# Pairing the score products and the transposes of two units in the first three attentions of a four-layer gated cross-attention model

## The chip, the cores and the metric

The kernel runs on one core of a Trainium2 chip. The metric is the time of one execution on the device, in microseconds; it is given as the median of several executions. The profile and the trace come from one further execution.

## The reference

Four layers, each a gated cross-attention and a gated feed-forward part, on an input x of 4 x 256 tokens with 128 features and a context of the same shape:

```python
x = x + tanh(g_xattn[0]) * L0_xattn(layernorm(x), ctx, ctx, adj, mask, ...)
x = x + tanh(g_ffn[0])   * L0_ffn(layernorm(x), ...)
x = x + tanh(g_xattn[1]) * L1_xattn(layernorm(x), ctx, ctx, bias, padding, ...)
x = x + tanh(g_ffn[1])   * L1_ffn(layernorm(x), ...)
x = x + tanh(g_xattn[2]) * L2_xattn(layernorm(x), ctx, ctx, mask, padding, ...)
x = x + tanh(g_ffn[2])   * L2_ffn(layernorm(x), ...)
x = x + tanh(g_xattn[3]) * L3_xattn(ctx, layernorm(x), ...)
x = x + tanh(g_ffn[3])   * L3_ffn(layernorm(x), ...)
```

The first three attentions have the same form, with 16 heads of 8 features, and differ in what is added to the scores and masked:

```python
q = heads(query @ Wq.T + bq); k = heads(key @ Wk.T + bk); v = heads(value @ Wv.T + bv)
scores = einsum('bhqd,bhkd->bhqk', q, k) * 8 ** -0.5 + bias        # 256 x 256 for each batch and head
weights = softmax(where(masked, -inf, scores), axis=-1)
out = einsum('bhqk,bhkd->bhqd', weights, v)                        # then @ Wo.T + bo
```

## The kernel before

The program is written out by hand for five engines, each of which issues its own list of instructions in order and waits for the others on semaphores. The stages follow one another: attention, feed-forward, and so on. The change concerns `attention(a)` of TensorE for a = 0, 1, 2.

In each of these attentions the work is cut into 64 units, one for each batch and head (`UNITS`; a group is four units with four heads of one batch, a batch is 16 units). A loop runs over steps t, on each engine with the same numbering, and in step t each engine does its part for a unit that lies a fixed number of steps back:

- TensorE, unit t: two score matmuls in bf16 of 128 x 256 each (line 998) into one of three PSUM banks (`SBANK`). They wait until VectorE is through with unit t - 3, which had the same bank.
- VectorE, unit t: adds the mask and bias and takes the negated row maximum, two custom instructions that write SBUF (line 1444).
- ScalarE, unit t: the exponential with the row sum, two instructions of 128 x 256 (line 715).
- TensorE, unit t - 3 (`LAG`): four transposes of the exponentials in f32 (line 1018) into one of three further banks (`TBANK`). They wait for the exponentials of that unit and for the copy of the unit that had the bank.
- Copy of the transposed unit t - 3 from PSUM to SBUF, by VectorE (line 1456), and for every fourth unit (those with number 2 in their group) by ScalarE (line 727).
- TensorE, every fourth step from 8 on (`PV_T`) and the step behind it: the product with V of a group, in two parts of four matmuls of 32 x 256 (line 1033). The first part waits until all four units are copied and until ScalarE has emptied the only bank for it.
- ScalarE, every fourth step from 9 on (`OTR_T`): copy of that product out of its bank (line 735).
- TensorE, every fourth step from 13 on (`SEL_T`): eight small matmuls that spread the reciprocal row sums (line 1050); VectorE multiplies the two (line 1466).
- TensorE and VectorE, at steps 27, 43, 59 and 75 (`OUT_T`), once for each batch: the output projection (lines 1061 and 1064) and its addition to x (line 1351).

The order within one step is the order of this list. Since each engine's list is in order, an instruction that waits holds back all that stands behind it. The lines that set the three lags and the banks:

```python
LAG, PV_T, OTR_T, SEL_T, OUT_T = 3, 8, 9, 13, 27
def SBANK(n):
    return bank[(0, 1, 7)[n % 3]]
def TBANK(n):
    return bank[(2, 3, 5)[n % 3]]
def loop_rings(ra, rb):
    return Ring((6,), s_fa, s_ea, ra.n, ra.n), Ring((4,), s_fb, s_eb, rb.n, rb.n)
```

Of the kernel before, what the change touches and what calls it, by code (L numbers as in the profile page):

```python
# [46 lines left out]
UNITS = 64  # L47
# [71 lines left out]
LAG, PV_T, OTR_T, SEL_T, OUT_T = 3, 8, 9, 13, 27  # L119
# [7 lines left out]
def program(nc, x_in, ctx_in, ctxT_in, w_in, adj_in, mask_in, pad_in, wint_in, out):  # L127
    with ExitStack() as stack:  # L128
# [719 lines left out]
        def _(pe):  # L848
# [87 lines left out]
            def attention(a):  # L936
                three = a == 3
                base = UNITS * a
                if not three:
                    if a == 0:  # L940
                        keys(0)
                    for c in range(NC):
                        bk = ra.fill(pe)
                        for i in range(4):
                            t = 4 * c + i
# [37 lines left out]
                la, lb = loop_rings(ra, rb)  # L983
                otr_at = {}
                for t in range(UNITS + SEL_T):
                    if t < UNITS:
                        n = base + t
                        b, j, g = t // 16, t % 4, t // 4 % 4
                        if n >= 3:

                            pe.wait_ge(s_max, 2 * n - 4)
                        bk = SBANK(n)
                        if t % 16 == 0:

                            pe.wait_ge(s_qs[min(b, 2)], 32 * (a + 1))
                        h = 4 * g + j
                        for q in range(2):
                            mm = nc.tensor.matmul(bk[:, q * S:(q + 1) * S],  # L998
                                                  QS[:, h, b * S + q * P:b * S + (q + 1) * P],
                                                  KS[:, h // 2, b * S:(b + 1) * S], start=True, stop=True)  # L1000
                        mm.then_inc(s_s, 1)
                    u = t - LAG
                    if 0 <= u < UNITS:
                        n = base + u
                        pe.wait_ge(s_exp, 2 * n + 2)
                        if n >= 3:

                            m = n - 3
                            if m % 4 == 2:
                                pe.wait_ge(s_te, m // 4 + 1)  # L1010
                            else:
                                pe.wait_ge(s_to, m // 4 * 3 + min(m % 4 + 1, 3))
                        bk = TBANK(n)
                        for kt in range(2):
                            for q in range(2):
                                o = kt * S + q * P
                                i = q * S + kt * P
                                mm = nc.tensor.transpose(bk[:, o:o + P], P_OF(n)[:, i:i + P], ident)  # L1018
                        mm.then_inc(s_t, 1)
# [936 lines left out]
```

## Time and profile before

| | us |
|---|---|
| median of 3 executions | 953.72 (953.38 to 954.16) |
| profiled execution | 955.74 |
| its span, first to last instruction | 954.0 |
| TensorE busy | 739.0 (77%) |
| VectorE busy | 629.7 (66%) |
| ScalarE busy | 531.1 (56%) |
| GpSimd busy | 211.9 (22%) |
| mean granted TensorE clock | 0.879 |

The shares are averages over stages that differ. The three loops of the change lie at 43.8 to 138.7, 188.6 to 283.2 and 564 to 659 us of the trace, some 285 us of the 954. Within a stage, an engine's idle time counts only where the others wait for it. A row of the trace in order of time gives the start, the duration from the first to the last of the instructions merged in it, engine, line, operation and tiles, the number of instructions, and in brackets the idle time of the engine just before and what ended it. The granted clock is a share of 2.4 GHz, so that 0.50 is 1.2 GHz. A matmul of f32 that is no transpose counts as two instructions in the trace, and as one in the listing of the program further down.

### The profile page before, as it was taken

The page shows a single profiled execution, that of the slowest core. Times are in us where ns is not written, and L with a number is a line of the kernel's source. Part 1 is how long each engine was busy: PE and PEld are TensorE (multiplying, and loading weights), DVE is VectorE, ACT ScalarE, POOL GpSimd, SP SyncE. Part 2 cuts the span into 40 slices and gives each one's busy share as a digit, 9 for nine tenths or more (in the row PEclk, how much of TensorE's full clock was granted, in tenths as well). Part 3 has the DMA queues.
Part 4 walks back from the last instruction along what each step waited for, and adds up shares of the span by engine and source line. Part 5 has one row for each costly group of instructions (what it writes and reads, how often), then busy time and mean ns, then how long its engine had stood idle before and what let it go on. Part 6 is the DMA issues. An engine that isn't in the chain of part 4 may idle for free. (4 is left out here: it accounts for less than half of the span.)

```text
span 954.0 us, 14468 instructions
## 1 busy us (share of the span) xinstructions
PE 739.0 (77%) x4720; PEld 415.6 (44%) x4720; DVE 629.7 (66%) x1861; ACT 531.1 (56%) x1376; POOL 211.9 (22%) x161
## 2 busy tenths in 40 slices
PE   4599973399975776877783559995899999969987
PEld 2266652166653222322331236664533666644322
DVE  3699957399963557686786569986532656634543
ACT  2398841198843775775674149882367655522211
POOL 7702004100004345364364630001010000000000
PEclk9699995599995987888896759998899999988999
DMA  7992040420000000000000190000000000000000
GB/s 285 181 345 68 3 67 1 103 31 2 2 2 0 0 1 0 0 1 0 1 0 0 26 173 2 2 3 23 1 0 1 1 1 1 1 0 1 1 0 23
DMA packets 22060, 32.29 MB, mean 34 GB/s; under 512 B 1761, under 2 KB 15713, under 8 KB 21217
## 3 DMA queue, kind: packets, MB, share of 16 engines
q1 hardware_dynamic: 21984, 31.36, 13.1%
q8 instruction: 39, 0.64, 0.3%
q14 instruction: 37, 0.29, 0.1%
HBM read 21.39 MB, written 9.96 MB: 33 GB/s over the span
## 5 line engine op out<-in xcount | busy, mean ns | idle before, releaser
L715 ACT ACTIVATE RING<-RING,NMX 128x256 f32<-128x256 f32 x384 | 190.6, 500 | 54.1 <-DVE NMX L1444 53.5
L1444 DVE CUSTOM_DVE_ANT_0 RING<-bank,ADJM 128x256 f32<-128x256 f32 x384 | 143.4, 413 | 22.7 <-DMA scratch<-RING 21.7
L1018 PE MATMUL bank<-W,RING 128*128 128x128 f32 x768 | 120.3, 281 | 15.7 <-ACT RING L727 14.0
L495 POOL TENSOR_TENSOR small<-small 128x8 f32<-128x8 f32 (+2 forms) x13 | 17.6, 1360 | 463.8 <-DVE small L1335 463.8
L1018 PEld LDWEIGHTS bank<-W,RING 128*128 128x128 f32 x768 | 91.3, 145 | 28.1 <-ACT RING L715 24.5
L998 PE MATMUL bank<-ARENA 128*128 128x256 bf16 x384 | 77.5, 289 | 28.8 <-DMA ARENA<-scratch 23.6
L1456 DVE COPY RING<-bank 128x512 f32<-128x512 f32 x144 | 98.6, 686 | 1.2 <-PE bank L1018 0.8
L857 PE MATMUL bank<-XT,W 128*128 128x512 f32 (+3 forms) x138 | 78.0, 706 | 7.2 <-ACT XT L611 5.1
L857 PE MATMUL bank<-ARENA 128*128 128x512 f32 (+2 forms) x164 | 62.2, 522 | 23.8 <-DVE ARENA L1537 10.2
L857 PE MATMUL bank<-ARENA,W 128*128 128x512 f32 (+4 forms) x104 | 54.4, 648 | 27.7 <-DVE ARENA L1657 10.9
L590 POOL TENSOR_TENSOR ARENA<-ARENA,RING 128x512 f32<-128x512 f32 x38 | 59.8, 1583 | 67.4 <-DVE RING L1627 35.5
L715 ACT ACTIVATION_READ_ACCUMULATOR RING<-RING,NMX 128x1 f32 x384 | 72.8, 190 | 0.0
L627 ACT ACTIVATE RING<-bank,NMX 128x512 f32<-128x512 f32 x64 | 43.4, 683 | 41.9 <-PE bank L922 21.2
L1033 PE MATMUL bank<-RING,ARENA 128*32 128x256 f32 x768 | 60.7, 390 | 2.7 <-DVE RING L1456 2.5
L1376 DVE TENSOR_REDUCE NMX<-bank 128x1 f32<-128x512 f32 x64 | 39.4, 678 | 31.9 <-PE bank L889 31.9
L1595 DVE TENSOR_SCALAR RING<-bank,W 128x512 f32<-128x512 f32 x36 | 27.0, 751 | 48.7 <-PE bank L1126 46.6
L998 PEld LDWEIGHTS bank<-ARENA 128*128 128x128 bf16 x384 | 31.1, 102 | 63.7 <-issue 38.0
L1126 PE MATMUL bank<-ARENA 128*128 128x512 f32 x72 | 39.4, 690 | 18.2 <-DVE RING L1602 15.0
L857 PEld LDWEIGHTS bank<-ARENA 128*128 128x128 f32 (+1 forms) x164 | 28.2, 196 | 55.3 <-issue 27.0
L857 PEld LDWEIGHTS bank<-XT,W 128*128 128x128 f32 (+2 forms) x138 | 26.9, 219 | 44.6 <-issue 23.6
L857 PEld LDWEIGHTS bank<-ARENA,W 128*128 128x128 f32 (+4 forms) x104 | 17.2, 186 | 66.2 <-issue 24.2
L842 ACT ACTIVATE RING<-bank 128x512 f32<-128x512 f32 x24 | 14.3, 597 | 56.6 <-PE bank L857 41.9
(240 smaller groups left out, 1395.6 us busy)
## 6 DMA issues: line engine op xcount, KB each, us to landing
scratch<-ARENA SPq DMA_DIRECT2D x18, 256.0 KB, 3.1
ARENA<-scratch SPq DMA_DIRECT2D x6, 768.0 KB, 10.6
W<-in_weights SPq DMA_DIRECT2D x1, 2564.0 KB, 21.2
scratch<-RING SPq DMA_DIRECT2D x36, 64.0 KB, 3.2
ARENA<-scratch SPq DMA_DIRECT2D x12, 192.0 KB, 3.7
scratch<-RING SPq DMA_DIRECT2D x18, 128.0 KB, 2.7
ARENA<-scratch SPq DMA_DIRECT2D x6, 384.0 KB, 7.0
W<-in_weights SPq DMA_DIRECT2D x2, 1024.0 KB, 13.8
```

The costliest lines, as they stand in the source:

```text
L590: nc.gpsimd.tensor_tensor(acc[:, half(c)], acc[:, half(c)], term, ALU.add).then_inc(s_sum, 1)
L627: nc.scalar.activation(LP_OF(u), bank[j][:, :], ACT.Exp, bias=NMX[:, u:u + 1], accum_out=SUMS[:, u:u + 1]).then_inc(l_exp, 1)
L715: nc.scalar.activation(P_OF(n)[:, q * S:(q + 1) * S], S_OF(n)[:, q, :], ACT.Exp, bias=NMX[:, 2 * t + q:2 * t + q + 1], scale=-1.0, accum_o ...
L857: mm = nc.tensor.matmul(bk[0:m, 0:rhs.shape[-1]], lhsT, rhs, start=(i == 0), stop=(i == len(terms) - 1))
L998: mm = nc.tensor.matmul(bk[:, q * S:(q + 1) * S], QS[:, h, b * S + q * P:b * S + (q + 1) * P], KS[:, h // 2, b * S:(b + 1) * S], start=Tru ...
L1018: mm = nc.tensor.transpose(bk[:, o:o + P], P_OF(n)[:, i:i + P], ident)
L1033: mm = nc.tensor.matmul(pv[PAD * j:PAD * j + PAD, 0:S], V[:, 2 * b + part, f:f + PAD], PT_OF(base + 4 * G + j)[:, part * S:(part + 1) * S] ...
L1126: nc.tensor.matmul(bank[u % 3][:, :], *control(u, 1), start=True, stop=True).then_inc(s_fs, 1)
L1376: nc.vector.tensor_reduce(NMX[:, u:u + 1], bank[j][:, :], AX.X, ALU.max, negate=True).then_inc(l_max, 1)
L1444: nc.vector.tensor_tensor_reduce(out=S_OF(n)[:, q, :], in0=SBANK(n)[:, q * S:(q + 1) * S], in1=ADJM[:, b, q, :], scale=-1.0, scalar=BIG, o ...
L1456: nc.vector.tensor_copy(PT_OF(n), TBANK(n)[:, :]).then_inc(s_to, 1)
L1595: nc.vector.tensor_scalar(SP_OF(u), bank[u % 3][:, :], be2[:, u % (NE + 1), 1:2], CLAMP, ALU.add, ALU.min).then_inc(s_mn, 1)
```

## The change

The score matmuls of units t and t + 1 are both issued in the even step t, and none in odd steps. The transposes, which in step t were those of unit t - 3, are now issued in odd steps only, for the units t - 4 and t - 3. All waits stay the same for each unit; the other engines' lists are not changed. Everything else in a step stays in its place, so the first part of a group's product with V, which falls into an even step, now directly follows the scores.

```diff
                 for t in range(UNITS + SEL_T):
-                    if t < UNITS:
-                        n = base + t
-                        b, j, g = t // 16, t % 4, t // 4 % 4
+                    for v in (t, t + 1) if t % 2 == 0 and t < UNITS else ():
+                        n = base + v
+                        b, j, g = v // 16, v % 4, v // 4 % 4
                         if n >= 3:
 
                             pe.wait_ge(s_max, 2 * n - 4)
                         bk = SBANK(n)
-                        if t % 16 == 0:
+                        if v % 16 == 0:
...
-                    u = t - LAG
-                    if 0 <= u < UNITS:
+                    for u in (t - 4, t - 3) if t % 2 == 1 else ():
+                        if not 0 <= u < UNITS:
+                            continue
                         n = base + u
                         pe.wait_ge(s_exp, 2 * n + 2)
```

The following listings show TensorE's matmuls in the order of the program: L998 are scores (two for a unit), L1018 transposes (four for a unit), L1033 the products with V, L1050 the spreading of the row sums. The change adds a line, so these are L1019, L1034 and L1051 in the second listing of each pair.

First, TensorE at the start of the first loop, before:

```order
L998 MATMUL bank<-ARENA 128x256 x8
L1018 MATMUL bank<-W,RING 128x128 x4
L998 MATMUL bank<-ARENA 128x256 x2
L1018 MATMUL bank<-W,RING 128x128 x4
L998 MATMUL bank<-ARENA 128x256 x2
L1018 MATMUL bank<-W,RING 128x128 x4
```

and after:

```order
L998 MATMUL bank<-ARENA 128x256 x8
L1019 MATMUL bank<-W,RING 128x128 x4
L998 MATMUL bank<-ARENA 128x256 x4
L1019 MATMUL bank<-W,RING 128x128 x8
L998 MATMUL bank<-ARENA 128x256 x4
L1019 MATMUL bank<-W,RING 128x128 x8
```

The transposes of unit 1 stood behind the scores of unit 4 and now stand behind those of units 4 and 5; those of unit 3 stood behind unit 6's scores and now stand behind units 6's and 7's.

Second, TensorE in a full group of four units (steps 4m to 4m + 3), before:

```order
L998 MATMUL bank<-ARENA 128x256 x2
L1018 MATMUL bank<-W,RING 128x128 x4
L1033 MATMUL bank<-RING,ARENA 32x256 x4
L998 MATMUL bank<-ARENA 128x256 x2
L1018 MATMUL bank<-W,RING 128x128 x4
L1033 MATMUL bank<-RING,ARENA 32x256 x4
L1050 MATMUL bank<-W,SUMS 32x128 x8
L998 MATMUL bank<-ARENA 128x256 x2
L1018 MATMUL bank<-W,RING 128x128 x4
L998 MATMUL bank<-ARENA 128x256 x2
L1018 MATMUL bank<-W,RING 128x128 x4
```

and after:

```order
L998 MATMUL bank<-ARENA 128x256 x4
L1034 MATMUL bank<-RING,ARENA 32x256 x4
L1019 MATMUL bank<-W,RING 128x128 x8
L1034 MATMUL bank<-RING,ARENA 32x256 x4
L1051 MATMUL bank<-W,SUMS 32x128 x8
L998 MATMUL bank<-ARENA 128x256 x4
L1019 MATMUL bank<-W,RING 128x128 x8
```

The first part of the product with V stood behind the transposes of the group's first pair and now stands ahead of them; in both halves of the group one unit's scores have passed one unit's transposes.

Third, TensorE behind the last scores of the first loop, before:

```order
L998 MATMUL bank<-ARENA 128x256 x2
L1018 MATMUL bank<-W,RING 128x128 x8
L1033 MATMUL bank<-RING,ARENA 32x256 x4
L1018 MATMUL bank<-W,RING 128x128 x4
L1033 MATMUL bank<-RING,ARENA 32x256 x4
L1050 MATMUL bank<-W,SUMS 32x128 x8
L1018 MATMUL bank<-W,RING 128x128 x4
```

and after:

```order
L998 MATMUL bank<-ARENA 128x256 x4
L1019 MATMUL bank<-W,RING 128x128 x8
L1034 MATMUL bank<-RING,ARENA 32x256 x4
L1019 MATMUL bank<-W,RING 128x128 x8
L1034 MATMUL bank<-RING,ARENA 32x256 x4
L1051 MATMUL bank<-W,SUMS 32x128 x8
L1019 MATMUL bank<-W,RING 128x128 x4
```

The transposes of unit 61 stood ahead of the first product here and now stand behind it, with those of unit 62.

## Rows read from the trace of the kernel before

**Rows 1.** Stretch: length, busy us PE, PEld, DVE, ACT, POOL, granted clock. First loop, its start.
```profile
43.80:138.70 94.90, 86.28 (x970) 62.61 (x970) 83.09 (x344) 77.96 (x288) 12.00 (x8) 0.96 0.46 129
43.80:50.60 6.80, 5.44 (x25) 4.53 (x26) 6.06 (x29) 5.98 (x24) 5.65 (x4) 0.50 1.18 181
```

**Rows 2.** Waits of VectorE in the first loop: total us, times, longest.
```profile
DVE XN L1466 <- PE bank L1050: 4.6, 7, 1.6
```

**Rows 3.** VectorE in order of time, steps 33 to 38: start, us, instruction.
```profile
86.81 0.42 DVE L1466 TENSOR_TENSOR XN<-XT,bank 128x256 f32<-128x256 f32 x1
...
91.76 0.42 DVE L1466 TENSOR_TENSOR XN<-XT,bank 128x256 f32<-128x256 f32 x1
92.11 0.42 DVE L1444 CUSTOM_DVE_ANT_0 RING<-bank,ADJM 128x256 f32<-128x256 f32 x1
...
92.81 0.69 DVE L1456 COPY RING<-bank 128x512 f32<-128x512 f32 x1
```

**Rows 4.** TensorE in order of time, steps 36 to 39.
```profile
88.65 0.63 PE L1018 MATMUL bank<-W,RING 128*128 128x128 f32 x4 [0.92 <-ACT RING L727]
89.21 0.64 PE L1033 MATMUL bank<-RING,ARENA 128*32 128x256 f32 x8
89.78 0.39 PE L998 MATMUL bank<-ARENA 128*128 128x256 bf16 x2
90.01 0.60 PE L1018 MATMUL bank<-W,RING 128*128 128x128 f32 x4
90.54 0.64 PE L1033 MATMUL bank<-RING,ARENA 128*32 128x256 f32 x8
90.99 0.62 PE L1050 MATMUL bank<-W,SUMS 128*32 128x128 f32 x16
91.55 0.39 PE L998 MATMUL bank<-ARENA 128*128 128x256 bf16 x2
91.78 0.60 PE L1018 MATMUL bank<-W,RING 128*128 128x128 f32 x4
92.21 0.38 PE L998 MATMUL bank<-ARENA 128*128 128x256 bf16 x2
```

**Rows 5.** ScalarE in order of time, steps 33 and 34.
```profile
87.93 0.58 ACT L727 ACTIVATE RING<-bank 128x512 f32<-128x512 f32 x1
88.41 0.37 ACT L735 ACTIVATE XT<-bank 128x256 f32<-128x256 f32 x1
...
89.56 0.19 ACT L715 ACTIVATION_READ_ACCUMULATOR RING<-RING,NMX 128x1 f32 x1
```

**Rows 6.** TensorE and VectorE in order of time at the starts of the loops.
```profile
49.23 0.63 PE L998 MATMUL bank<-ARENA 128*128 128x256 bf16 x2
49.66 1.06 PE L1018 MATMUL bank<-W,RING 128*128 128x128 f32 x4
...
193.01 0.69 DVE L1456 COPY RING<-bank 128x512 f32<-128x512 f32 x1
...
194.59 0.42 DVE L1444 CUSTOM_DVE_ANT_0 RING<-bank,ADJM 128x256 f32<-128x256 f32 x1 [0.21 <-ACT RING L715]
...
568.45 1.06 PE L1018 MATMUL bank<-W,RING 128*128 128x128 f32 x4
```

**Rows 7.** TensorE and VectorE in order of time around the second batch end.
```profile
100.83 0.61 DVE L1351 SCALAR_TENSOR_TENSOR X<-bank,small,X 128x128 f32<-128x128 f32 x2 [1.02 <-PE bank L1064]
...
103.26 0.62 PE L1050 MATMUL bank<-W,SUMS 128*32 128x128 f32 x16
...
103.95 0.42 DVE L1466 TENSOR_TENSOR XN<-XT,bank 128x256 f32<-128x256 f32 x1 [0.55 <-PE bank L1050]
```

**Rows 8.** TensorE and VectorE in order of time behind the last scores.
```profile
128.06 0.64 PE L1033 MATMUL bank<-RING,ARENA 128*32 128x256 f32 x8
...
128.63 0.66 PE L1018 MATMUL bank<-W,RING 128*128 128x128 f32 x4
...
130.91 0.69 DVE L1456 COPY RING<-bank 128x512 f32<-128x512 f32 x1
```

## The prediction

> **What bounds the kernel now.** I read the busy time of the first attention loop first, then the waits of VectorE in it, then the order of time on three engines in one group of four units, then the same at the loop's start, at a batch end and at its end. Units are named by number: S(n) the two score matmuls, M(n) VectorE's mask-add-and-minimum, E(n) ScalarE's exponentials, T(n) the four transposes, C(n) the copy to SBUF, PV0 and PV1 the two halves of a group's product with V, SEL the product that spreads the row sums, OTN VectorE's multiplication behind it.
>
> The loop of the first attention takes 94.90 us, in which VectorE is busy 83.09, TensorE 86.28 and ScalarE 77.96 [rows 1]; the two other loops look alike. VectorE hardly waits inside it: 4.6 us in seven waits for SEL [rows 2], and 1.02 us at each of the three batch ends inside the loop [rows 7]. The rest of its idle time lies behind the last scores. So between the batch ends **VectorE sets the pace**, one group of four units in 4.95 us (OTN at 86.81 to OTN at 91.76, with M directly behind, [rows 3]), and TensorE only has to be in time. It just is: SEL starts at 90.99, an OTN can start 0.69 behind a SEL (103.26 and 103.95, [rows 7]), so 91.68, and does at 91.76; S(38) starts at 91.55 and M(38), which needs it complete, at 92.11 [rows 3, 4]. A group in which TensorE comes later than now is therefore paid in full, one in which it comes earlier brings nothing, except where VectorE waits for it.
>
> **The change part by part.** No instruction is added or taken away. Of every two steps the order S(2k), T(2k-3), S(2k+1), T(2k-2) becomes S(2k), S(2k+1), T(2k-3), T(2k-2); so S(2k+1) passes one T, and PV0, which stood behind T(2k-3), now stands ahead of it.
>
> *Full groups.* Take steps 36 and 37. Before: T(33) at 88.65, 0.14 behind the copy of unit 30 on ScalarE (87.93 and 0.58), then PV0 0.56 later, S(37) 0.57, T(34) 0.23, PV1 0.53, SEL 0.45 [rows 4, 5]. Now S(37) goes into the 0.92 us that TensorE idles ahead of T(33); it waits for M(34) only, which directly follows the OTN at 86.81 and is through some 1.1 us behind it. PV0 comes next, and needs its bank emptied: ScalarE's copy for the group before ends at 88.41 + 0.37 = 88.78 [rows 5]. With the same 0.14, PV0 starts at 88.92, T(33) 0.57 later (PV0 to T(62) is 0.57 in [rows 8]) at 89.49, T(34) 0.43 later at 89.92 (T(35) to S(39) is 0.43, [rows 4]; E(34) is complete at 89.56 + 0.19 = 89.75, so that wait is hidden), PV1 0.53 later at 90.45, SEL 0.45 later at 90.90. That is **0.09 earlier** than 90.99. T(35) then starts at 90.90 + 0.56 + 0.23 + 0.23 = 91.92 and ends 0.60 later at 92.52, while its copy starts at 92.81 [rows 3]: hidden, with 0.3 left. T(33) ends at 90.1, 0.8 later than before; its copy comes one step behind that of unit 32 and not before 90.4: hidden, with 0.3 left. So full groups cost 0.
>
> The 0.14 is a handoff from ScalarE to TensorE as the row shows it. The Trainium skill (Advanced Engine Details and Errata, Network/Comms) gives 50 to 100 ns for reading a semaphore; by that PV0 would start at 88.83 to 88.88, the chain would be 0.04 to 0.09 shorter still, and the sum below 0.4 to 0.9 us lower. The sum takes 0.14.
>
> *Where VectorE waits.* The batch result's matmuls start when the same T(4m) is through as before, so the 0.09 is gained in each of 3 x 3 waits of 1.02, and in the first of the seven waits for SEL: 10 x 0.09 = **0.9 us gained**. Behind a batch end TensorE issues S(44), S(45), PV0, T(41), T(42), PV1, SEL in place of S(44), T(41), PV0, S(45), T(42), PV1, SEL: the same pieces. C(41), which followed M(44) at once, comes some 0.44 later, but VectorE then waits 0.55 for SEL anyway [rows 7], so this is hidden, and only just. Bounds: 0 to 1.8.
>
> *Start of the loops.* There TensorE runs at 1.2 GHz (granted clock 0.50 in the first 6.80 us, and with 0.96 over the whole loop it is 1.00 behind them, [rows 1]) and is the slower engine. T(1) and T(3) now stand behind one more pair of scores, 0.43 at that clock (49.23 to 49.66, [rows 6]). First loop: T(3) starts at 50.09 in place of 49.66 and runs partly at 2.4 GHz, since the clock rises at 50.6. All at the low clock it would end 0.43 later, all at the high one (0.60 for 1.06) 0.03 earlier; I take 0.24 for it and for C(3) directly behind. Second loop: C(1), at 193.01, comes 0.41 later; two steps further the wait of 0.21 ahead of M(6) at 194.59, and what is idle beside it, swallow 0.2 to 0.3 of that. I take 0.15. Third loop: T(1) starts 0.43 behind 568.45, at 568.88, and meets the rising clock too, so some 0.17. Nothing behind these gives them back, since the stalls further on are reached through the same engines. Together 0.24 + 0.15 + 0.17 = **0.6 us**, between 0 and 1.2.
>
> *End of the loops.* In step 64 the order is PV0, T(61) where it was T(61), PV0. PV0 starts at 128.06, behind a copy on VectorE that does not move, and T(61) used to be done by then (the pair T(60), T(61) stood ahead). Now T(61) stands between PV0 and T(62), and everything behind it (T(62) at 128.63, PV1, SEL, T(63), C(63) at 130.91) comes 0.43 later [rows 8]. E(63) does not hold it: it follows M(63), which is not moved. Behind C(63) all is one chain up to the next layer's normalisation. 3 x 0.43 = **1.3 us**, and I see no cover: bounds 1.2 to 1.3.
>
> Sum: 1.3 + 0.6 - 0.9 = +1.0 us. The profiled execution took 955.74 us (span 954.0), 2.02 more than the median of 953.72; the sum is a difference, so I forecast 956.7 for a profiled execution and **954.7 for the median**. A measurement of this kernel tells about 0.2% from no change, which is 1.9 us; so this is no change that can be told.
>
> **The rivals.**
>
> *PV0 hands over late (slower).* PV0 now gates T, T, PV1 and SEL, and it waits for the last thing that ScalarE does in its group. If the handoff is above 0.14 + 0.09 = 0.23, SEL and S(38) come later than now and VectorE pays in every full group. At 0.30 it is 0.07 in each of 12 groups x 3, 2.5 us; the 0.9 gained at batch ends is gone and 9 x 0.07 = 0.6 is lost there: 1.0 + 0.9 + 2.5 + 0.6 = +5.0, so 958.7. For it: slack behind S(38) is nil, and T(34) has only 0.17 to spare behind E(34). Against it: both waits for ScalarE in [rows 4, 5] end 0.14 behind it. 18 in 100.
>
> *The pieces pack more tightly (faster).* A T followed by PV takes 0.53, followed by S 0.43; PV followed by a waiting S takes 0.57, by SEL 0.45 [rows 4]. If in the new order the 0.10 and the 0.12 fall away around PV0, the chain to a batch end and the one from it to SEL each lose 0.22: 9 x 0.44 = 4.0 us more gained, so +1.0 - 4.0 = -3.0, 950.7. For it: [rows 7] show the places at which it would count. Against it: the 0.57 also stands in front of a T in [rows 8]. 10 in 100.
>
> *The clock falls.* Were the new pauses of TensorE (at most 0.7 us, where today's are 0.92) to drop it to 1.2 GHz in the loops, the pair of scores would take 0.43 as in [rows 6] in place of 0.23 as in [rows 4], all else twice as long too, and a group's own chain of some 4.4 us (4 x 0.66 for S and T, 1.76 for the rest) 8.8 in place of VectorE's 4.95: 48 x 3.9 = 185 us more, 1140. The Trainium skill (TensorE: Matmul & The Clock Gate, A second HAM failure mode: psum-queue depth-cycling) says that short idles between groups of matmuls that cycle through banks can make the clock swing; by that rule this rival would be the outcome. The trace stands against it: the granted clock stays at 1.00 behind the loop's start [rows 1], with such idles in every group. 1 in 100.
>
> *Clock edges move.* The clock rises at another point of each loop's start and of the stages between, since the pauses around it shift by some tenths. Three starts at one bound or the other are 1.2 us apart, and the stages between have such edges too. up to 1.5 us either way, the width of my forecast.
>
> **How the numbers follow.** The forecast has 71 in 100: of these 55 within 0.2%, 11 above (starts at their upper bound and no gain at the batch ends: 1.3 + 1.2 = 2.5) and 5 below. With the rivals: faster by over 0.2% 5 + 10 = 15, within 55, slower 11 + 18 + 1 = 30. The range goes down to 952.4 and up to 958.0; it leaves out most of the tight packing, the upper half of the late handoff and the clock, about 19 in 100.
>
> **What would show it.** In the profile after: C(63) to the loop's end unchanged but C(63) about 0.4 later behind PV0; T(61) and T(62) in one row of eight; in full groups OTN to OTN still 4.95 and no wait on VectorE; PV0 0.14 behind ScalarE's copy of the bank; batch-end waits of 0.9 in place of 1.02; behind a batch end a wait of VectorE ahead of C(41) in place of part of that for SEL. Wrong if VectorE waits for SEL, scores or transposes in groups where it does not now, or if the loops are shorter than before.

## The result, and the profile after

The changed kernel took a median of 955.04 us (952.91 to 958.23, 20 runs), the kernel before on the same chips 953.62 us (951.15 to 954.48, 20 runs). The ratio is 1.002 with an interval of 1.0011 to 1.0030: some 1.0 to 2.9 us slower, 1.9 by the ratio itself and 1.4 by the medians. The forecast of 954.7 us holds within half a microsecond. Its second half, "no change that can be told", does not quite: the interval excludes no change, though the loss is no larger than the 0.2% that the prediction took as its bound for telling one.

The profiled execution of the changed kernel has a span of 953.0 us, one less than before (954.0), at a mean granted clock of 0.881 (0.879 before). The busy times on the profile's page are nearly those of before (739.0, 415.6, 629.7, 531.1 and 211.9 us):

```profile
PE 739.4 (78%) x4715; PEld 417.3 (44%) x4720; DVE 630.7 (66%) x1861; ACT 530.0 (56%) x1376; POOL 211.8 (22%) x161
```

A shorter span and a longer median do not contradict each other. The stages that the change does not touch took 3.4 us less in this one execution than in that of before, and the three loops 2.4 us more. The untouched stages run the same program in both, so their difference is scatter between executions. The loops must therefore be read on their own. I cut each loop at VectorE's rows, by start times: from its first mask instruction to the first batch result (the addition to x, line 1351, now 1352), from there to the third batch result, and from there to the last.

| us | to the first batch result, loops 1 / 2 / 3 | first to third | third to last | sum of three loops |
|---|---|---|---|---|
| before | 34.82 / 34.55 / 34.24 | 44.39 | 15.09 | 282.06 |
| after | 35.20 / 34.62 / 34.62 | 44.42 | 15.58 | 284.46 |

The two middle columns are the same in all three loops to within 0.02. So the +2.40 consist of +0.83 in the stretches that hold the starts, 3 x 0.03 in the middle, and 3 x 0.49 = +1.47 at the ends.

The changed kernel in the first loop (columns as in [rows 1]: stretch, length, busy time of PE, PEld, DVE, ACT, POOL, granted clock):

```profile
43.80:139.00 95.20, 86.96 (x970) 63.24 (x970) 82.96 (x343) 77.71 (x288) 11.90 (x8) 0.96 0.46 128
```

The clock is 0.96 as in [rows 1]; TensorE now idles ahead of PV0 and not ahead of T(33), and this did not lower it. Its waits (engine, tile and line that waited, what it waited for: total, times, longest), VectorE's and one of TensorE's:

```profile
DVE X L1352 <- PE bank L1065: 6.3, 4, 3.2
DVE XN L1467 <- PE bank L1051: 3.1, 3, 1.6
DVE RING L1457 <- PE bank L1019: 2.2, 6, 0.4
PE bank L1034 <- ACT XT L735: 3.8, 7, 0.9
```

The profile lists three waits of VectorE for SEL where it listed seven ([rows 2]), and six for transposes. It lists none under 0.15 us. One full group of four units, three engines in order of time (start, us from the first to the last of the merged instructions, engine, line, operation, tiles, count, idle before and what ended it):

```profile
87.00 0.42 DVE L1467 TENSOR_TENSOR XN<-XT,bank 128x256 f32<-128x256 f32 x1
...
88.59 0.37 ACT L735 ACTIVATE XT<-bank 128x256 f32<-128x256 f32 x1
...
89.11 0.64 PE L1034 MATMUL bank<-RING,ARENA 128*32 128x256 f32 x8 [0.55 <-ACT XT L735]
...
89.68 1.09 PE L1019 MATMUL bank<-W,RING 128*128 128x128 f32 x8
...
90.70 0.64 PE L1034 MATMUL bank<-RING,ARENA 128*32 128x256 f32 x8
...
91.15 0.62 PE L1051 MATMUL bank<-W,SUMS 128*32 128x128 f32 x16
91.71 0.61 PE L998 MATMUL bank<-ARENA 128*128 128x256 bf16 x4
91.95 0.41 DVE L1467 TENSOR_TENSOR XN<-XT,bank 128x256 f32<-128x256 f32 x1
```

OTN to OTN is 4.95 as before, and VectorE waits nowhere in it. PV0 waits for ScalarE's copy and starts 0.15 behind its end (88.59 + 0.37 = 88.96), 2.11 behind OTN, as forecast. SEL, however, is 4.15 behind OTN; it was 4.18 ([rows 3, 4]), and 4.09 was expected. The group behind this one takes 4.95 (91.95 to 96.90), where it took 4.97 before (91.76 to 96.74): in the kernel before M(38) waited 0.02 for its scores, which stand behind SEL, and now it does not. The earlier TensorE brings that much and no more.

A batch end:

```profile
100.99 0.61 DVE L1352 SCALAR_TENSOR_TENSOR X<-bank,small,X 128x128 f32<-128x128 f32 x2 [1.03 <-PE bank L1065]
...
101.99 1.09 PE L1019 MATMUL bank<-W,RING 128*128 128x128 f32 x8
...
102.69 0.69 DVE L1457 COPY RING<-bank 128x512 f32<-128x512 f32 x1 [0.41 <-PE bank L1019]
...
103.02 0.64 PE L1034 MATMUL bank<-RING,ARENA 128*32 128x256 f32 x8
...
103.47 0.62 PE L1051 MATMUL bank<-W,SUMS 128*32 128x128 f32 x16
...
104.16 0.42 DVE L1467 TENSOR_TENSOR XN<-XT,bank 128x256 f32<-128x256 f32 x1
```

The wait for the batch result is 1.03, where [rows 7] had 1.02. Behind it the wait of 0.55 for SEL is no longer listed and one of 0.41 for the transposes of the pair stands in its place: the copy of unit 41, which followed its mask instructions at once, now waits. SEL still holds OTN all the same. OTN starts 0.69 behind SEL (103.47 to 104.16) as in [rows 7], with 0.10 of waiting left, too short for the list. OTN comes 3.17 behind the batch result, where it came 3.12, because SEL comes 2.48 behind it and not 2.43 ([rows 7]).

Behind the last scores of the loop:

```profile
128.31 0.64 PE L1034 MATMUL bank<-RING,ARENA 128*32 128x256 f32 x8 [0.58 <-DVE RING L1457]
128.88 1.09 PE L1019 MATMUL bank<-W,RING 128*128 128x128 f32 x8
129.90 0.64 PE L1034 MATMUL bank<-RING,ARENA 128*32 128x256 f32 x8
130.35 0.62 PE L1051 MATMUL bank<-W,SUMS 128*32 128x128 f32 x16
...
131.60 0.69 DVE L1457 COPY RING<-bank 128x512 f32<-128x512 f32 x1
```

The transposes of units 61 and 62 are one row of eight between the two products, and the last copy comes 131.60 - 128.31 = 3.29 behind PV0, where it came 130.91 - 128.06 = 2.85 ([rows 8]): 0.44 later.

### The profile page after: what moved, and what is told of

The parts are those of the page before. It is cut to its first block and busy times, and to the rows that moved or that the text cites. A ratio compares the mean times of both kernels' runs of the same rounds, so it can differ in the third digit from the quotient of the medians.

```text
span 953.0 us, 14463 instructions
## 1 busy us (share of the span) xinstructions
PE 739.4 (78%) x4715; PEld 417.3 (44%) x4720; DVE 630.7 (66%) x1861; ACT 530.0 (56%) x1376; POOL 211.8 (22%) x161
## 5 line engine op out<-in xcount | busy, mean ns | idle before, releaser
L1019 PE MATMUL bank<-W,RING 128*128 128x128 f32 x768 | 107.0, 283 | 1.6 <-ACT RING L715 1.6
L1019 PEld LDWEIGHTS bank<-W,RING 128*128 128x128 f32 x768 | 88.2, 145 | 23.0 <-ACT RING L715 17.8
L998 PE MATMUL bank<-ARENA 128*128 128x256 bf16 x384 | 64.3, 289 | 28.3 <-DMA ARENA<-scratch 22.9
L1034 PE MATMUL bank<-RING,ARENA 128*32 128x256 f32 x768 | 60.7, 389 | 18.1 <-ACT XT L735 11.5
L998 PEld LDWEIGHTS bank<-ARENA 128*128 128x128 bf16 x384 | 33.3, 102 | 50.6 <-issue 31.8
```

Of the source, the lines that this page charges most:

```text
L998: mm = nc.tensor.matmul(bk[:, q * S:(q + 1) * S], QS[:, h, b * S + q * P:b * S + (q + 1) * P], KS[:, h // 2, b * S:(b + 1) * S], start=Tru ...
L1034: mm = nc.tensor.matmul(pv[PAD * j:PAD * j + PAD, 0:S], V[:, 2 * b + part, f:f + PAD], PT_OF(base + 4 * G + j)[:, part * S:(part + 1) * S] ...
```

## The experiments

My theory said where the time goes: into the starts, where TensorE is still slow and is the bound, and into the ends, where all is one chain; full groups were to cost nothing, and the batch ends to give a little back. The rivals put it into the full groups or the clock. Each experiment changes nothing but the order of TensorE's list. Ratios are against the kernel before, run on the same chip, and need not be the quotient of two medians. The stretches are those of the table above, from one profiled execution of each kernel. The middle and the last stretch repeat to 0.02 us in the three loops of an execution; the starts do not. The intervals of most ratios overlap, so which part of the order costs what is read from the stretches, and the ratios only confirm the size.

| kernel | median us | ratio (interval) | starts, loops 1 / 2 / 3 | first to third | third to last | loops |
|---|---|---|---|---|---|---|
| end single | 955.29 | 1.0010 (1.0000 to 1.0021) | 34.47 / 34.75 / 34.50 | 44.42 | 15.47 | 283.39 |
| full groups only | 954.93 | 1.0008 (0.9995 to 1.0020) | 34.44 / 34.77 / 34.77 | 44.43 | 15.46 | 283.67 |
| scores only | 952.71 | 0.9995 (0.9984 to 1.0006) | 34.38 / 34.24 / 34.21 | 44.20 | 15.13 | 280.82 |
| transposes only | 958.27 | 1.0043 (1.0028 to 1.0058) | 35.05 / 35.49 / 35.54 | 44.69 | 15.54 | 286.76 |
| single from 60 | 954.02 | 1.0009 (0.9999 to 1.0019) | 34.97 / 34.61 / 34.59 | 44.42 | 15.14 | 282.86 |
| scores from 8 | 954.07 | 1.0004 (0.9991 to 1.0016) | 34.24 / 33.97 / 33.95 | 44.20 | 15.14 | 280.16 |
| product behind pair | 956.60 | 1.0037 (1.0025 to 1.0050) | 35.09 / 35.24 / 35.22 | 44.48 | 15.40 | 285.20 |
| scores and late product | 948.93 | 0.9958 (0.9941 to 0.9974) | 33.96 / 33.96 / 33.95 | 43.61 | 14.98 | 277.64 |
| late product only | 951.08 | 0.9983 (0.9969 to 0.9997) | 34.82 / 34.80 / 34.24 | 43.90 | 14.97 | 280.46 |

### The end alone undone

On the changed kernel, transposes of one unit per step once the scores are through:

```diff
-                    for u in (t - 4, t - 3) if t % 2 == 1 else ():
+                    for u in (t - 3,) if t >= UNITS else (t - 4, t - 3) if t % 2 == 1 else ():
```

> The change, but behind the last scores (steps 64 on) TensorE issues the transposes as before: T(61) ahead of PV0. Loop lengths are from the first mask-and-minimum of VectorE to the last addition to x, summed over the three loops: 282.06 us before, 284.46 after the change. Theory (the cost lies at the starts and ends of the loops, full groups are free): the end is back at its old length, 0.49 less in each loop, sum 283.0; in time about +0.9 us over the kernel before in place of +1.4 to +2.4. Rival (the cost is spread over the full groups and batch ends): the sum stays at 284.0 or more. Rival (nothing but scatter): no length moves by a fixed amount.

The last stretch came down from 15.58 to 15.47 only, not to 15.09, and the sum to 283.39, not to 283.0, so my account of the end was not complete. TensorE behind the last scores of the first loop, and ScalarE's last steps before it:

```profile
125.72 0.51 ACT L715 ACTIVATE RING<-RING,NMX 128x256 f32<-128x256 f32 x1 [0.69 <-DVE NMX L1445]
...
126.72 0.57 ACT L727 ACTIVATE RING<-bank 128x512 f32<-128x512 f32 x1
...
127.44 0.63 PE L1019 MATMUL bank<-W,RING 128*128 128x128 f32 x4 [0.30 <-ACT RING L727]
128.00 0.64 PE L1034 MATMUL bank<-RING,ARENA 128*32 128x256 f32 x8
```

The transposes of unit 61 stand ahead of PV0 again, but now they are late themselves: they wait for the bank that ScalarE copies out (126.72 and 0.57), and PV0 waits behind them. ScalarE is late because of the third batch end, at step 60. There the pair's transposes come behind PV0, VectorE waits 0.4 us for them as in the batch end shown above, and ScalarE behind it waits 0.69 for VectorE (125.72), where the kernel further down that undoes the order from step 60 on waits 0.19. From there to unit 58's copy ScalarE has no idle time left to make this good. In the changed kernel this cannot be seen, since PV0 does not stand behind a copy of ScalarE there. The end thus had **two covers for one loss**: lifting one shows the other.

### Only the full groups changed

In addition, scores and transposes of single units up to step 7:

```diff
-                    for v in (t, t + 1) if t % 2 == 0 and t < UNITS else ():
+                    for v in (t,) if t < 8 else (t, t + 1) if t % 2 == 0 and t < UNITS else ():
-                    for u in (t - 3,) if t >= UNITS else (t - 4, t - 3) if t % 2 == 1 else ():
+                    for u in (t - 3,) if t < 8 or t >= UNITS else (t - 4, t - 3) if t % 2 == 1 else ():
```

> Pairs only from step 8 to step 63, the first eight steps and all behind step 63 as before. Theory: both costs are gone, the sum of the loop lengths is 282.1 (within 0.3), the time that of the kernel before within 0.1%; the wait of VectorE behind a batch end still stands ahead of its copy (0.40) and no longer at the multiplication. Rival (spread over groups and batch ends): 283.5 to 284.5.

The sum, 283.67, missed the 282.1 of the theory and lies where the rival had it. The rival is wrong all the same: the middle, which holds the full groups and batch ends, is 44.43 against 44.39, 0.12 in three loops. The end is 15.46, as in the run before, which makes 1.1. The starts look no better in the table (34.44, 34.77, 34.77, against 34.82, 34.55, 34.24 of the kernel before, which has the same order there), so start stretches of single executions can't be compared as they stand: the clock's rise falls at another point each time. For each start, the table gives how long the granted clock stayed at 1.2 GHz behind the first mask, and how far the first OTN lies behind that mask:

| order up to step 7 | us at 1.2 GHz, and first mask to first OTN |
|---|---|
| single (before, this kernel, late product) | 4.33: 15.18; 4.47: 15.18; 5.32: 15.40; 5.42: 15.48; 6.76: 15.74; 6.85: 15.75; 6.93: 15.73; 7.33: 15.73; 7.41: 15.76 |
| both paired (after, end single, single from 60) | 4.34: 15.42; 4.44: 15.46; 4.62: 15.55; 4.65: 15.57; 5.19: 15.57; 5.24: 15.57; 6.29: 15.70; 6.75: 15.92; 7.38: 16.15 |

Two things are in it. A clock that rises 3 us later costs a start 0.55 us in the single order (15.18 to 15.73) and 0.73 in the paired one (15.42 to 16.15). And at nearly the same rise the paired order costs 0.2 to 0.4 more: 0.24 at 4.3 us, 0.28 at 4.4, 0.17 at 5.2 to 5.3, 0.18 at 6.8 and 0.39 at 7.4. The mean is 0.25, so my estimate for three starts is 0.75 us; the 0.83 of the table hold a little of the clock's scatter too.

### One half of the change at a time

Scores paired, transposes single:

```diff
-                    for u in (t - 4, t - 3) if t % 2 == 1 else ():
+                    for u in (t - 3,):
```

> Only the scores are paired; the transposes stand in their old steps, so PV0 is behind T(33) again and S(37) no longer between PV0 and T(34). Theory: TensorE reaches the row-sum product 0.18 earlier in a full group, which brings nothing, since VectorE sets the pace (4.95 us a group); the starts cost what they cost in the change (0.8 in all), the ends nothing: sum 282.9, time +0.8 us over before. Rival (an earlier TensorE is worth something in each group): a sum below 281.

The full groups take 4.95, the wait for the batch result is 0.92, the middle is 44.20 and the end 15.13. Group and batch end of this kernel, TensorE and VectorE:

```profile
86.33 0.42 DVE L1467 TENSOR_TENSOR XN<-XT,bank 128x256 f32<-128x256 f32 x1
...
90.36 0.62 PE L1051 MATMUL bank<-W,SUMS 128*32 128x128 f32 x16
...
91.28 0.42 DVE L1467 TENSOR_TENSOR XN<-XT,bank 128x256 f32<-128x256 f32 x1
...
100.21 0.61 DVE L1352 SCALAR_TENSOR_TENSOR X<-bank,small,X 128x128 f32<-128x128 f32 x2 [0.92 <-PE bank L1065]
```

SEL is 4.03 behind OTN, 0.15 earlier than in the kernel before, and the wait for the batch result is 0.10 shorter: what I had forecast for the whole change (0.09 in each) does happen, with this half. In the groups themselves 0.02 is gained, in the one of four that took 4.97. The sum of 280.82 missed the 282.9 of the theory and lies under the 281 of the rival, but not for the rival's reason. Of the 1.24 less than before, 0.57 are in the middle, from the shorter waits for the batch result, and 0.78 in the starts (the ends take 0.12 more). In the starts the clock rose earlier in this execution (5.53, 4.38 and 4.31 us behind the first mask, against 6.85, 5.42 and 4.33 before). What the paired scores cost a start is read further down.

Then transposes paired, scores single:

```diff
-                    for v in (t, t + 1) if t % 2 == 0 and t < UNITS else ():
+                    for v in (t,) if t < UNITS else ():
```

> Only the transposes are paired; S(37) stands between PV0 and T(33). PV0 still waits for ScalarE's copy of its bank, and now S, T, T, PV1 and the row-sum product follow it: that product comes about 0.2 us later than in the kernel before. Theory (TensorE is just in time, later is paid in full): 0.12 to 0.19 in each of some 40 groups, 5 to 7 us, beside the 2.3 of starts and ends: sum 289 to 292, time +7 to +10 us, groups of 5.1 in place of 4.95, and VectorE waits for the row-sum product in full groups. Rival (there is slack in the groups): sum 284.5, as the change.

This is the rival in which TensorE is late in a full group, made to happen:

```profile
86.59 0.42 DVE L1467 TENSOR_TENSOR XN<-XT,bank 128x256 f32<-128x256 f32 x1
...
90.92 0.62 PE L1051 MATMUL bank<-W,SUMS 128*32 128x128 f32 x16
91.61 0.42 DVE L1467 TENSOR_TENSOR XN<-XT,bank 128x256 f32<-128x256 f32 x1
92.04 0.42 DVE L1445 CUSTOM_DVE_ANT_0 RING<-bank,ADJM 128x256 f32<-128x256 f32 x1
...
95.87 0.62 PE L1051 MATMUL bank<-W,SUMS 128*32 128x128 f32 x16
96.66 0.42 DVE L1467 TENSOR_TENSOR XN<-XT,bank 128x256 f32<-128x256 f32 x1
```

SEL is 4.33 behind OTN (86.59 to 90.92), 0.15 later than before. OTN follows 0.69 behind it, 5.02 behind the last and 0.07 later than the 4.95 of before; the other 0.08 had been slack. They are paid one instruction further: M(38) starts 0.43 behind OTN (91.61 to 92.04) and not 0.35 ([rows 3]), since its scores stand behind the late SEL. So the group that begins there takes 5.05 in place of 4.97, although its own SEL (95.87) does not hold the next OTN, which follows 0.79 behind it. Together the lateness of 0.15 is paid in full, as the prediction said of a late group. But it is paid once in a batch, over two groups. The group behind a batch end has slack (5.06 before, 5.05 here), the group that holds the next batch end waits for the batch result anyway, and the middle rose by 0.30 in two batches, not by the several microseconds that I had expected. The sum of 286.76 thus lies between the theory (289 to 292) and the rival (284.5). The ratio of 1.0043 (4.1 us) agrees with the loops (+4.70).

### The end once more, single from step 60 on

If both covers are known, undoing the pairs from the third batch end on must give the end back:

```diff
-                    for u in (t - 4, t - 3) if t % 2 == 1 else ():
+                    for u in (t - 3,) if t >= 60 else (t - 4, t - 3) if t % 2 == 1 else ():
```

> The change, but from step 60 on the transposes stand in their old steps (in the run before this only from step 64 on, which left the end at 15.47 us, from the third batch result to the last, against 15.09 before and 15.58 with the change). Theory: the end has two covers that the change takes away one by one. Behind the third batch end the transposes of unit 57 come late, VectorE and through it ScalarE fall back by 0.4, and ScalarE's copy of unit 58 then holds back the product and all behind it; undoing the order from step 60 removes both: end 15.1 to 15.2. Middle (first to third batch result) unchanged at 44.42. Rival (undoing the end never helps, the 0.4 come from the scores of units 61 and 63 being early): end 15.45 as in the run before.

TensorE and ScalarE, where the run above had its wait of 0.30:

```profile
126.40 1.48 PE L1019 MATMUL bank<-W,RING 128*128 128x128 f32 x12
126.53 0.58 ACT L727 ACTIVATE RING<-bank 128x512 f32<-128x512 f32 x1
128.01 0.64 PE L1034 MATMUL bank<-RING,ARENA 128*32 128x256 f32 x8
```

Three units' transposes run in one piece, with no wait among them. The last stretch is 15.14, against 15.58 changed and 15.09 before. So 0.44 of the end's 0.49 come from the transposes paired in steps 60 to 65.

### Scores paired, but not at the start

On the changed kernel:

```diff
-                    for v in (t, t + 1) if t % 2 == 0 and t < UNITS else ():
+                    for v in (t,) if t < 8 else (t, t + 1) if t % 2 == 0 and t < UNITS else ():
-                    for u in (t - 4, t - 3) if t % 2 == 1 else ():
+                    for u in (t - 3,):
```

> Candidate that may beat both: scores paired from step 8 on, the first eight steps and all transposes as in the kernel before. Theory: middle 44.20 as in the run with only the scores paired (44.39 before), end 15.13 (15.09 before), start as before at the same length of the slow clock (first row-sum multiplication 15.2 to 15.8 us behind the first mask, by when the clock rises). Each loop 0.2 to 0.3 us shorter than before, 0.7 us in all, 0.9993: at or under what can be told. Rival: no shorter than before, 1.0000 or above, because the start gives it back.

The loops are the shortest so far (280.16, 1.9 less than before), and the ratio of 1.0004 with an interval from 0.9991 to 1.0016 does not show it. It only excludes a gain above 0.9 us. This is the one kernel whose loops and ratio differ by more than 1.5 us. Part of the 1.9 is the clock's: it rose 5.37, 4.59 and 4.53 us behind the first mask here, and 6.85, 5.42 and 4.33 before. The third loop's start, at nearly the same rise, is 0.29 shorter (33.95 against 34.24); with that for each start my estimate of the gain is 3 x (0.29 + 0.19 - 0.05) = 1.3 us. That is still above what the timing allows, and I leave it at that: a gain of this size is at the edge of what these runs can tell.

The starts can be priced here once more, since this kernel differs from the one with only the scores paired in the first eight steps alone. The first OTN lies 15.31, 15.03 and 15.03 us behind the first mask here, and 15.45, 15.32 and 15.28 there, with rises at 5.53, 4.38 and 4.31. The scores paired in steps 0 to 7 thus cost a start 0.14 to 0.29 us, 0.66 in the three loops: the larger part of what the change costs at the starts, and the mechanism that the prediction named, one more pair of scores ahead of the first transposes.

### Both products behind the pair

On the changed kernel, PV0 goes behind the pair of transposes, so that those need not wait for ScalarE's copy of its bank:

```diff
-                    if k >= 0 and k % 4 <= 1 and k // 4 < UNITS // 4:
+                    for part in (0, 1) if k >= 0 and k % 4 == 1 and k // 4 < UNITS // 4 else ():
-                        G, part = k // 4, k % 4
+                        G = k // 4
```

> The change, with the first half of the product with V moved behind the pair of transposes, so both halves are issued in the odd step. T(34) then waits for its exponentials (2.94 us behind the multiplication of the group before, so it starts at 3.09), the product at 3.62, the row-sum product at 4.48, where it was 4.18 before, 4.15 in the change and 4.26 with only the transposes paired. Theory (what exceeds 4.18 is paid in full in the groups that have no batch end): 0.30 in each of two or three groups of a batch, and the batch end: middle 45.6 to 46.8 in place of 44.42, the three loops 6 to 10 us longer than before, time +6 to +10. Rival (VectorE and ScalarE shift along, so that the cycle does not lengthen by the full delay): middle under 45.2.

```profile
86.44 0.41 DVE L1467 TENSOR_TENSOR XN<-XT,bank 128x256 f32<-128x256 f32 x1
...
89.44 0.66 PE L1019 MATMUL bank<-W,RING 128*128 128x128 f32 x4 [0.53 <-ACT RING L715]
90.02 1.07 PE L1034 MATMUL bank<-RING,ARENA 128*32 128x256 f32 x16
90.91 0.62 PE L1051 MATMUL bank<-W,SUMS 128*32 128x128 f32 x16
91.60 0.42 DVE L1467 TENSOR_TENSOR XN<-XT,bank 128x256 f32<-128x256 f32 x1
...
100.74 0.35 DVE L1352 SCALAR_TENSOR_TENSOR X<-bank,small,X 128x128 f32<-128x128 f32 x1 [1.03 <-PE bank L1065]
...
103.62 0.42 DVE L1467 TENSOR_TENSOR XN<-XT,bank 128x256 f32<-128x256 f32 x1 [0.30 <-PE bank L1051]
```

The middle of 44.48 is neither the 45.6 to 46.8 of the theory nor, in its reason, the rival's "under 45.2". The groups are worse, by what the theory said of one of them: the second transposes of the pair now wait for the exponentials with both products behind them, SEL is 4.47 behind OTN, 0.29 later than before, and OTN to OTN takes 5.16 and 5.06 in place of 4.95 and 4.97. As with the transposes alone, that is the lateness paid in full, but once in a batch. But behind a batch end the same order takes 2.88 from batch result to OTN (100.74 to 103.62), where the changed kernel takes 3.17 and the one before 3.12. There the transposes' data are long ready, and what counts is how quickly VectorE gets them and how tightly the pieces pack; the two products in one row take 0.89 up to SEL (90.02 to 90.91), where the changed kernel has 0.57 behind the one and 0.45 behind the other (89.11 to 89.68, 90.70 to 91.15). The gain at the batch ends nearly pays for the groups. What is left of the 3.1 us in the loops lies in the starts (1.9) and the ends (0.9).

### The late product only where it pays

So I took from this only the group behind a batch end, on top of the kernel with the scores paired from step 8:

```diff
+                    late = t % 16 in (12, 13) and t > 16
-                    if k >= 0 and k % 4 <= 1 and k // 4 < UNITS // 4:
+                    for part in (((), (0, 1)) if late else ((0,), (1,)))[k % 4] if k >= 0 and k % 4 <= 1 and k // 4 < UNITS // 4 else ():
-                        G, part = k // 4, k % 4
+                        G = k // 4
```

> Built from what the runs so far showed: scores paired from step 8 on, transposes one by one, and in the first two steps behind a batch end (44 and 45, 60 and 61, and 28 and 29) both halves of the product behind the two transposes. In the run with the product behind the pair the stretch from a batch result to the next multiplication took 2.88 us, where it takes 3.12 before and 3.17 in the change; with only the scores paired the stretch from a multiplication to the batch result took 3.98 where it takes 4.09. Theory: both gains hold together, a batch in the middle takes 22.10 - 0.29 = 21.8 us (22.20 before), the three loops 282.06 - 3 x (0.14 + 2 x 0.39 + 0.25) = 278.6, time -3.4 us, ratio 0.9964. Rival (the copy of unit 41 or the exponentials become late, or the full groups behind give it back): middle of 44.2 as with the scores alone, ratio 0.999 to 1.000.

The median is 948.93 us (947.61 to 952.97), a ratio of 0.9958 (0.9941 to 0.9974): faster than the kernel before, and so than the changed kernel, which was not run beside it. The loops give 282.06 - 277.64 = 4.4 us, the ratio 4.0 (2.5 to 5.6). Part of the 4.4 is again the clock's, which rose early in all three loops (4.54, 4.68 and 4.43 us). With the third start's 0.29 for each, my estimate is 3 x (0.29 + 0.78 + 0.11) = 3.5 us, against the 3.4 of the theory. A batch end of this kernel, TensorE and VectorE:

```profile
99.61 0.61 PE L998 MATMUL bank<-ARENA 128*128 128x256 bf16 x4
99.72 0.61 DVE L1353 SCALAR_TENSOR_TENSOR X<-bank,small,X 128x128 f32<-128x128 f32 x2 [0.92 <-PE bank L1066]
100.06 1.04 PE L1019 MATMUL bank<-W,RING 128*128 128x128 f32 x8
...
101.03 1.07 PE L1035 MATMUL bank<-RING,ARENA 128*32 128x256 f32 x16
101.92 0.62 PE L1052 MATMUL bank<-W,SUMS 128*32 128x128 f32 x16
...
102.60 0.42 DVE L1468 TENSOR_TENSOR XN<-XT,bank 128x256 f32<-128x256 f32 x1 [0.30 <-PE bank L1052]
```

From the scores' start to SEL it is 2.31 (99.61 to 101.92). In the kernel before, the same six pieces in their old order take 2.54: the scores behind the second batch end start at 100.72 there, and SEL at 103.26 ([rows 7]). Batch result to OTN is 2.88, 0.24 less than before; with the shorter wait for the batch result (0.92), a batch takes 43.61 / 2 = 21.80 in place of 22.20.

And the late product by itself, the same lines on the kernel before:

> The kernel before with the late product behind batch ends alone: S, T, S, T, PV0, PV1 in place of S, T, PV0, S, T, PV1. Theory: 0.24 less behind each batch end, nothing elsewhere: middle 43.9 in place of 44.39, the three loops 2.2 us shorter, ratio 0.9977. Rival (the gain needs the scores paired): middle 44.3 to 44.4, ratio 1.000.

The ratio is 0.9983 (0.9969 to 0.9997), the middle 43.90 and the end 14.97; the loops are 1.6 us shorter, not 2.2, with later rises of the clock (7.41, 6.76 and 4.47 us) than before. So of the 0.39 per batch of the combination, 0.245 are the late product's. The paired scores bring the other 0.145. Without the late product they brought 0.095 (44.20), since a transpose then stands directly behind PV0 at the batch end, and with the transposes paired as well nothing (44.42). On the same chip the combination is 2.1 us faster than the late product alone by the medians, but the two intervals overlap.

## Why the prediction was right, and which steps were not

**The number.** The sum came out within 0.4 us of the medians, and in part by luck. It counted 0.9 us of gain that did not come; without it, it would have been +1.9. The profiled loops lost 2.4.

**Bound, full groups: right.** "VectorE sets the pace": 4.95 in every version in which TensorE is not late, though SEL moved by 0.15. An earlier TensorE brought 0.02 in one group of four and not nothing. Its lateness is paid in full: SEL 0.15 late cost 0.07 and 0.08 in two groups.

**Batch ends, -0.9: this step failed.** The middle of the three loops measured +0.1 instead of a gain. The step said that SEL comes 0.09 earlier, "T(33) 0.57 later, T(34) 0.43 later, PV1 0.53 later". The first pitch is right (89.11 to 89.68), but the pair from its start to PV1 takes 1.02 (89.68 to 90.70) and not 0.96, and the same 1.02 stands at the end of the loop (128.88 to 129.90). Windows that begin inside the pair show why. TensorE of the changed kernel, the pair behind PV0 from its first, second and third transpose on, then the pair behind scores from its first and second:

```profile
89.68 1.09 PE L1019 MATMUL bank<-W,RING 128*128 128x128 f32 x8
89.84 0.93 PE L1019 MATMUL bank<-W,RING 128*128 128x128 f32 x7
89.95 0.82 PE L1019 MATMUL bank<-W,RING 128*128 128x128 f32 x6
...
92.15 1.04 PE L1019 MATMUL bank<-W,RING 128*128 128x128 f32 x8
92.26 0.93 PE L1019 MATMUL bank<-W,RING 128*128 128x128 f32 x7
```

The first transpose directly behind a product with V takes 0.16 before the second starts, the next 0.11, and behind scores the first takes 0.11 too. With that, only 0.03 of the 0.09 are left. The group ahead of the one with the batch end takes 0.02 of it (4.97 to 4.95), so nothing is left for the wait for the batch result, which measured 1.03. In the old order no transpose stands directly behind a product within a group. At the end of the loop one does, and the rows had it: four transposes took 0.66 there ([rows 8]) and 0.60 behind scores ([rows 4]). I used the start of that row and did not read its length. Behind a batch end the copy of unit 41 waits 0.41. That was forecast as "hidden, and only just", and it is hidden: OTN comes 0.05 later there because SEL does, with a pair of transposes directly behind PV0, the same 0.05 again. In the kernel with the pairs undone from step 60 on, the copy behind the third batch end no longer waits, and OTN is as late. That the mechanism existed is shown by the kernel with the scores alone: SEL 0.15 earlier, 0.10 off the wait.

**Starts, +0.6: right in place, somewhat small.** The profiled executions show 0.83, and at equal clock I estimate 0.75. That clock edges move a start by 0.55 to 0.73 makes 1.7 to 2.2 for three, above the 1.5 either way that I had allowed.

**Ends, +1.3: right in size, with a cover unseen.** Measured 3 x 0.49 = 1.47. T(61) between PV0 and T(62) costs 0.44 by the rows above. The other part, some 0.05, is what is left when the pairs from step 60 on are undone (15.14 against 15.09). The scores stay paired there, and T(58) stands directly behind PV0. "I see no cover" was wrong in the other direction: had T(61) stayed ahead of PV0, the end would still have been 0.38 late, because the pair at the third batch end makes ScalarE late. The bounds of 1.2 to 1.3 were too narrow for a sum of which one row had been read.

**Sum.** +2.4 in the loops against a forecast of +1.0. The difference of 1.4 is the 0.9 that were not gained, 0.1 lost in the middle instead, 0.2 in the starts and 0.2 at the ends. Timed, it is +1.4 by the medians and 1.0 to 2.9 by the ratio.

**Rivals.** PV0 hands over 0.15 behind ScalarE, so the late handoff did not happen; its price was also set too high, since a lateness is paid once in a batch and not in each full group (the run with the transposes alone). The Trainium skill (Advanced Engine Details and Errata, Network/Comms) gives 50 to 100 ns for reading a semaphore. The trace shows 0.15 us from the end of ScalarE's copy to the first matmul, more than the read alone, and the row was the right one to sum with. The tighter packing did not come in the change, but it exists in another order: two products in one row, which made the faster kernel. The clock did not fall: 0.96 over the loop as before, with idles of 0.5 to 0.6 us in each group. The Trainium skill (TensorE: Matmul & The Clock Gate, A second HAM failure mode: psum-queue depth-cycling) tells of a clock that swings under short idles between groups of bf16 matmuls of N = 512. This case, with f32 matmuls and bf16 ones of N = 256, does not show it.

One thing stays open: whether pairing the scores from step 8 on, with nothing else, gains. The loops say 1.9 us, some 1.3 at equal clock, the timing no more than 0.9. On top of the late product the paired scores took another 2.1 us off the median.

## What to carry to other kernels

Where one engine sets the pace and another only has to be in time, reordering the second is worth next to nothing in the steady state, as long as it stays in time. Its price and its worth lie where the pipeline fills, drains and stalls, and those places must be summed one by one, each with the order that is right for it. And when undoing a suspected loss gives back little, look for a second one under it before dropping the first.

## What the runs showed of the hardware

- A float32 transpose directly behind a product that uses 32 columns of the array (128*32 in the rows) took 0.16 us to the next one, behind bf16 scores or another transpose 0.11. At the full clock it was 0.16 to 0.17 at all 315 places behind a product in the traces of the eleven kernels, and 0.11 at 766 of the 790 behind scores. So a pair of units behind PV0 took 1.02, and 0.97 behind scores in the combination (100.06 to 101.03).
- TensorE started 0.14 to 0.15 us behind the end of the ScalarE copy it waited for, whether for transposes or for a product. Where it waited for the exponentials, it started 0.05 to 0.06 behind the end of ScalarE's read of the row sum.
- A rise of the granted clock 3 us later moved a loop's start by 0.55 us with single transposes and scores, and by 0.73 with both paired. That is more than the reordering itself cost there (0.17 to 0.39), so such stretches can only be compared at the same rise.
